# Step size of a state-space layer: the predicated copy stays on the Vector engine, the sum and the product move to GpSimd

## The reference

```
x = silu(causal_conv4(x_in))                    # 512 channels
dt, Bm, C = split(x @ x_proj_w.T)
dt = softplus(dt @ dt_proj_w.T + dt_proj_b)     # the step size
h = exp(dt * A) * h + dt * B * x                # 16 states per channel, over time
y = (h . C) + x * D ;  out = (y * silu(z)) @ out_proj_w.T
```

## Time and profile before

| what | value |
|---|---|
| time, median of 3 runs (lowest to highest) | 3368.63 us (3365.46 to 3370.95) |
| the profiled execution's own time | 3368.68 us |
| span in its trace, first to last instruction | 3367.0 us |
| busy: PE, DVE, ACT, POOL | 2878.9, 2203.8, 1425.5, 1199.6 us |
| mean granted TensorE clock | 0.909 of full speed |

### The profile page before, as it was taken

One profiled execution on the slowest core, in us unless ns is written; L12 is line 12 of the kernel. 1 busy time (PEld: TensorE's weight loads), 2 busy tenths in 40 slices (PEclk: granted clock), 3 DMA queues, 4 the chain that ended last, 5 costly groups with the idle time before them and its releaser, 6 DMA issues.

```text
span 3367.0 us, 45234 instructions
## 1 busy us (share of the span) xinstructions
PE 2878.9 (86%) x14054; PEld 1313.5 (39%) x14055; DVE 2203.8 (65%) x3070; ACT 1425.5 (42%) x2463; POOL 1199.6 (36%) x1360
## 2 busy tenths in 40 slices
PE   6994698888988988869999997878788888989876
PEld 5662133232332332236666665752222222222212
DVE  3576866766766767022222222646999999999997
ACT  2341065665655655712222221425445445545442
POOL 1143021221112212210000001825777767777675
PEclk9996598998988989979999998998898999998978
DMA  6166413133132130041111112620000000000000
GB/s 200 63 215 145 138 41 46 26 63 53 27 57 44 42 47 23 18 131 31 31 31 31 31 31 80 210 96 7 3 17 13 7 13 20 7 13 13 13 1 19
DMA packets 175061, 176.60 MB, mean 52 GB/s; under 512 B 50674, under 2 KB 151541, under 8 KB 174749
## 3 DMA queue, kind: packets, MB, share of 16 engines
q1 hardware_dynamic: 168732, 157.52, 18.7%
q0 software_dynamic: 6144, 16.82, 1.5%
HBM read 100.46 MB, written 73.83 MB: 52 GB/s over the span
## 4 chain that ended last, share of the span: by engine, by line
PE 50%; DVE 26%; issue 10%; ACT 5%; DMA 2%; POOL 2%; SPq 1%; another core or an unknown queue 1%; POOLq 0%; DVEq 0%; ACTq 0%; PEldq 0%
PE ps L1668 47%; DVE hh L1634 10%; DVE mp L1405 6%; DVE ps L1621 3%; POOL Ch L890 2%; PE ps L1876 2%; DMA ks<-qk_parts 1%; ACT Pt L1013 1%; DVE dt L1608 1%; DVE tl L1607 1%; DVE q L1317 1%; SPq L528 1%; PE ps L1832 1%; SPq L619 0%
## 5 line engine op out<-in xcount | busy, mean ns | idle before, releaser
L1405 DVE TENSOR_REDUCE mp<-ps 128x1 f32<-128x1024 f32 (+7 forms) x768 | 669.5, 909 | 276.0 <-PE ps L1668 245.7
L1013 ACT ACTIVATE Pt<-ps 128x512 f32<-128x512 f32 (+3 forms) x1280 | 611.6, 539 | 519.0 <-PE ps L1668 487.6
L890 POOL TENSOR_TENSOR Ch<-hh,Cb 128x1024 f32<-128x1024 f32 x256 | 603.7, 2358 | 72.6 <-DVE hh L1634 72.6
L1668 PE MATMUL ps<-ks,qs 96*128 96x512 bf16 (+3 forms) x1280 | 395.8, 382 | 117.8 <-DVE mp L1405 68.5
L1634 DVE TENSOR_TENSOR_SCAN hh<-dA,hst,ps 128x512 f32<-128x512 f32 x384 | 473.1, 1263 | 0.0
L766 POOL TENSOR_SCALAR_AFFINE_SELECT Pt<-Pt 128x128 f32<-128x128 f32 x512 | 147.8, 294 | 880.0 <-ACT Pt L1013 870.6
L1668 PE MATMUL ps<-dtx,pick 32*128 32x512 f32 x1024 | 326.0, 697 | 139.9 <-DVE hh L1634 139.1
L1668 PE MATMUL ps<-qs,ks 99*128 99x512 bf16 (+3 forms) x1280 | 413.3, 370 | 18.6 <-ACT Pt L1013 15.9
L1193 ACT ACTIVATE dA<-ps 128x1024 f32<-128x1024 f32 x256 | 261.8, 1023 | 392.4 <-PE ps L1668 392.1
L1621 DVE TENSOR_TENSOR ps<-ps,Bb 128x512 f32<-128x512 f32 x512 | 325.4, 680 | 32.9 <-PE ps L1668 32.4
L1668 PE MATMUL ps<-dt,WA 32*128 32x512 f32 x1024 | 322.0, 707 | 20.3 <-ACT dA L1193 20.1
(11 more groups left out here) (303 smaller groups left out, 3765.2 us busy)
## 6 DMA issues: line engine op xcount, KB each, us to landing
W<-in_L_ffn_w SPq DMA_DIRECT2D x16, 1024.0 KB, 12.0
qk_parts<-q SPq DMA_DIRECT2D x32, 384.0 KB, 2.9
qs<-qk_parts SPq DMA_DIRECT2D x96, 128.0 KB, 6.2
ks<-qk_parts SPq DMA_DIRECT2D x96, 128.0 KB, 8.7
expert_out<-yb SPq DMA_DIRECT2D x72, 128.5 KB, 2.5
expert_in<-zero SPq DMA_DIRECT2D x9, 1024.0 KB, 11.4
xg<-expert_in SPq DMA_DIRECT2D x72, 128.0 KB, 2.7
X<-in_L_attn_x SPq DMA_DIRECT2D x4, 1024.0 KB, 9.5
```

What stands on the lines that cost most here:

```text
L890: pool.tensor_tensor(Ch[:, k % 6, :, :], hh[:, k % HRING, :, :], Cb[:, par:par + 1, :].broadcast_to([P, 2, CH]), ALU.mult).then_inc(s_Ch, 1)
L1013: act.activation(Pt[:, n % PRING, q0:CH], ps[:, 4 + n % SRING, q0:CH], ACT.Exp, scale=SCALE).then_inc(s_exp, 1)
L1405: dve.tensor_reduce(mp[:, qc, h, t % TPC, k0 // 1024:k0 // 1024 + 1], slot[:, 0:n], AX.X, ALU.max).then_inc(s_free, 1)
L1668: return pe.matmul(o, lhsT, rhs, start=start, stop=stop, **kw)
```

## The change

`step_size` on the Vector engine shrinks to `select`, the predicated copy alone, at the same places. A new `step_size` on GpSimd does the sum and the product; it stands between the save of the state and the product with C in units 28, 0, 4, 8 (5, 9, 13 in chunk 0), and for the first block of all ahead of unit 0. A new semaphore `s_sel` goes from the one to the other. The three counters `s_nrm_abs`, `s_nrm_ps` and `s_sc`, each raised once, in that order, become one, `s_nrm`, awaited at 1, 2 and 3.

```diff
@@ GpSimd
+            def step_size(m, d):
+
+                par, b = m % 2, m * KI + d + 1
+                pool.wait_ge(s_sel, b)
+                pool.tensor_tensor(dt[:, par, d, :], dt[:, par, d, :], tl[:, d, :], ALU.add).then_inc(s_dt, 1)
+                pool.wait_ge(s_dt, b)
+                pool.wait_ge(s_xs, m + 1)
+                pool.tensor_tensor(dtx[:, par, d, :], dt[:, par, d, :], xs[:, par, d, :], ALU.mult).then_inc(s_dtx, 1)
...
             for step in range(2):
                 series(0, 0, step)
+            step_size(0, 0)
...
+                if n == 0 and u in (5, 9, 13):
+                    step_size(0, u // 4)
+                if n + 1 < NC and u == 28:
+                    step_size(n + 1, 0)
+                if n and u in (0, 4, 8):
+                    step_size(n, u // 4 + 1)
@@ ScalarE
-            act.activation(gb[:, :, :, :], ga[:, :, :, :], ACT.Abs).then_inc(s_nrm_abs, 1)
-
-            act.wait_ge(s_sc, 1)
-            act.wait_ge(s_nrm_ps, 1)
+            act.activation(gb[:, :, :, :], ga[:, :, :, :], ACT.Abs).then_inc(s_nrm, 1)
+
+            act.wait_ge(s_nrm, 3)
@@ Vector engine
-            def step_size(m, d):
-
-                par, b = m % 2, m * KI + d + 1
-                dve.wait_ge(s_mask, b)
-                dv.link(dve.copy_predicated(tl[:, d, :], te[:, d, :].bitcast(I32), dtx[:, par, d, :]))
-                dve.tensor_tensor(dt[:, par, d, :], dt[:, par, d, :], tl[:, d, :], ALU.add).then_inc(s_dt, 1)
-                dve.wait_ge(s_dt, b)
-                dve.wait_ge(s_xs, m + 1)
-                dve.tensor_tensor(dtx[:, par, d, :], dt[:, par, d, :], xs[:, par, d, :], ALU.mult).then_inc(s_dtx, 1)
+            def select(m, d):
+
+                dve.wait_ge(s_mask, m * KI + d + 1)
+                dve.copy_predicated(tl[:, d, :], te[:, d, :].bitcast(I32), dtx[:, m % 2, d, :]).then_inc(s_sel, 1)
```

More of the change, by code:

```diff
@@ L409, in build @@
         s_x, s_w, s_g = sem("s_x"), sem("s_w"), sem("s_g")
-        s_nrm_abs, s_nrm_ps, s_sc, s_scaled = sem("s_nrm_abs"), sem("s_nrm_ps"), sem("s_sc"), sem("s_scaled")
+        s_nrm, s_scaled = sem("s_nrm"), sem("s_scaled")
         s_hor, s_hev, s_sqp, s_sqe, s_fin, s_fev = (sem(n) for n in ("s_hor", "s_hev", "s_sqp", "s_sqe", "s_fin", "s_fev"))
@@ L445, in build @@
         s_jfull, s_jfree = sem("s_jfull"), sem("s_jfree")
-        s_xs, s_zs, s_ln, s_poly, s_mask, s_dt, s_dtx = (sem(n) for n in ("s_xs", "s_zs", "s_ln", "s_poly", "s_mask", "s_dt", "s_dtx"))
+        s_xs, s_zs, s_ln, s_poly, s_mask, s_sel, s_dt, s_dtx = (sem(n) for n in ("s_xs", "s_zs", "s_ln", "s_poly", "s_mask", "s_sel", "s_dt", "s_dtx"))
         s_dtb, s_dxb, s_dA, s_Bu, s_h, s_hst, s_Ch, s_red, s_yz, s_sum = (sem(n) for n in ("s_dtb", "s_dxb", "s_dA", "s_Bu", "s_h", "s_hst", "s_Ch", "s_red", "s_yz", "s_sum"))
@@ L1254, in _ @@
             dv = Chain(dve, c_dve)
-            dve.wait_ge(s_nrm_ps, 1)
+            dve.wait_ge(s_nrm, 2)
             dv.link(dve.tensor_reduce(nrm[:, 0:1], ps[:, 6:8, 0:512], AX.XY, ALU.max))
@@ L1260, in _ @@
             dv.link(dve.tensor_scalar(nri[:, 3:4], nri[:, 2:3], -1.0, 127.0, ALU.mult, ALU.add))
-            dve.tensor_single_scalar(nrm[:, 1:2].bitcast(I32), nri[:, 3:4], 23, ALU.logical_shift_left).then_inc(s_sc, 1)
+            dve.tensor_single_scalar(nrm[:, 1:2].bitcast(I32), nri[:, 3:4], 23, ALU.logical_shift_left).then_inc(s_nrm, 1)
             def statistics(k):
@@ L1643, in gate_y @@
                 dve.tensor_tensor(zs[:, n % 2, d, :], ps[:, 6, :], zs[:, n % 2, d, :], ALU.mult).then_inc(s_yz, 1)
-            step_size(0, 0)
+            select(0, 0)
             for k in range(NC * UNITS):
@@ L1650, in _ @@
                 if n == 0 and u in (5, 9, 13):
-                    step_size(0, u // 4)
+                    select(0, u // 4)
                 if n + 1 < NC and u == 28:
-                    step_size(n + 1, 0)
+                    select(n + 1, 0)
                 if n and u in (0, 4, 8):
-                    step_size(n, u // 4 + 1)
+                    select(n, u // 4 + 1)
                 if u in (11, 19, 27):
@@ L1674, in _ @@
             pe.wait_ge(s_const, 6 + TAYLOR)
-            pe.wait_ge(s_nrm_abs, 1)
+            pe.wait_ge(s_nrm, 1)
             for g in range(NROT + 1):
@@ L1678, in _ @@
                     last = mm(half(6 + g // 2, g % 2), ones_s[:, :], gb[:, min(g, NROT - 1), k, :], k == 0, k == KD - 1)
-            last.then_inc(s_nrm_ps, 1)
+            last.then_inc(s_nrm, 1)
             pe.wait_ge(s_scaled, 2)
```

## The result

The changed kernel takes 3340.45 us (median of 4 runs, 3336.55 to 3343.57); the kernel before, on the same chip, 3367.05 (3365.24 to 3370.95). The ratio is 0.9915, 95% interval 0.9903 to 0.9927: 0.85% or 27 to 29 us faster. Forecast were 45 us, with 3323 us as the likeliest time and 3300 to 3347 as the range. The direction and the place of the gain were right, its size was 1.5 to 1.7 times too large. The time lies inside the range, but 5 us above the 3307 to 3335 that had been given 60 in 100, and in the rival "half given back" (3335 to 3362).

A forecast was written before the change was run, and what follows sets the result against it. The Vector engine was taken as the bound, at 127 of 133 us in a chunk. 98.4 - 45.3 (copies) - 1.3 (start) - 3.5 (mask) - 3 (TensorE) = 45.3 us less, from 3368.7 to 3323 us; range 3300 to 3347.

The forecast's parts named there:

- the place of the gain: Last stage, Vector engine: taking sum and product, 69.8 us, from this bounding engine shortens the stage.
- half given back: Rival: new 3.4 us stall at unit 31 or 0 per chunk, or copies near 2.4 us; 3335 to 3362 us; 17 in 100.
- the counters: Three counters merged, one wait fewer on ScalarE: nothing won or lost that the measurement can tell (0.2%, 6.7 us).
- the mechanism of turns: Vector engine instructions with two SBUF inputs and GpSimd instructions reading SBUF exclude each other for their whole length.
- hidden waits for TensorE: TensorE loses 7 of its 18 us idle per chunk, so waits can surface; 3 us set, bounds nothing and 24.
- the slower rival: GpSimd becomes the bound through the ring of four `Ch`; some 3390 us; 4 in 100.
- the copy's term: Vector engine copies left: 24 at 1.6 us, seven of unit 28 at 0.88, the first 0.73; 45.3 us.
- full gain: Rival: copies stay near 0.8 us in gaps left by GpSimd's lag, nothing surfaces; 3293 to 3307 us; 15 in 100.
- a new stall of 3.4 us in each chunk: Second cause in a rival of 17 in 100: a stall at unit 31 or 0 of each chunk.
- The wait described for a short copy in unit 0: Unit 31's silu of z, covered by unit 0's 3.46 us step size; cover shrinks to 1.6; 0.4 us a chunk.
- The start: First block's step size, alone on the path: 2 x 0.69 becomes 2 x 1.27 and a hop between engines, +1.3 us.
- The mask: Block 3's mask waits for GpSimd's later half of unit 5, delaying unit 8's copy: 0.5 us in seven chunks, 3.5.

The follow-up runs named there:

- e3: Changed kernel without the predicated copy, its waits and signal kept; ratio 0.9833 to the kernel before, stage 1010.3 us.
- e9: Changed kernel without GpSimd's sum and product, only their signals kept; ratio 0.9837 to the kernel before, stage 1010.0 us.
- e4: Changed kernel with GpSimd's product with C as two instructions of 512 in every unit; ratio 0.9861 to the kernel before, stage 1020.1 us.
- e8: Changed kernel with the sum back on the Vector engine and GpSimd's product with C in two halves; ratio 0.9929 to the kernel before.

## Why the prediction was half right

Right: the counters (nothing); the place of the gain; both new instructions at 1.27 us; the mechanism of turns, by which a copy of 0.73 us waits out what GpSimd has begun; that GpSimd has hardly a pause from unit 28 to unit 8 (none between 2671.3 and 2723.0 us) but does not stop the scan (no wait of the scan for `Ch` in the trace after); that hidden waits for TensorE surface. Nothing in the trace speaks for the slower rival.

The step that failed is the size of the copy's term: "So a copy costs 0.72 + 0.88 = 1.6 us there. I take that for 24 copies". With the eight other copies it came to 45.3 us in the forecast; the trace has 59.0. The seven of unit 28 were as forecast but for one (0.74 to 1.69 us, together 6.7 against 6.2), the first 0.74; the 24 others took 51.5 us, 2.15 each in place of 1.6. I had taken the moment of the copy as random in a stretch in which GpSimd runs without a pause. It is not: ten of the 24 lie between 2.58 and 2.73 us, right behind the start of a product with C, the worst moment there is. The rival "full gain" had this objection in it, "the order of turns is fixed", with the wrong sign. Why the moment falls just there, right behind the start of a product, no run settles; one reason may be that both engines leave each collision together and then go through the same durations. The rival "half given back" came nearer: it named copies near 2.4 us. Its other cause, a new stall of 3.4 us in each chunk, did not come about as such.

Second, TensorE: 3 us were set, 9.4 measured, inside the bounds of 0 to 24. The wait described for a short copy in unit 0 appears in two of the seven chunks, 4 and 5, in units 3 and 4; these two make 6.5 of the 9.4 us. In chunk 5 the copy took 0.73 us, and the next units waited:

```profile
2941.89 0.73 DVE L1621 COPY_PREDICATED tl<-te,dtx 128x512 f32<-128x512 int32 x1
...
2954.19 0.69 DVE L1653 TENSOR_TENSOR zs<-ps,zs 128x512 f32<-128x512 f32 x1 [0.96 <-PE ps L1678]
...
2958.40 1.30 DVE L1631 TENSOR_TENSOR ps<-ps,Bb 128x512 f32<-128x512 f32 x2 [2.33 <-PE ps L1678]
```

In chunk 3, where it took 2.72 us, no wait follows in these units. But the copy's length does not decide it alone: in chunk 4 it took 2.29 us and 3.2 us of waits followed, in chunk 2 it took 2.22 us and none did. Why is open. As a sum, e3 and e9 show that copies cost less than they last: 59.0 us of them gone shorten the stage by 24.1, 30.7 gone by 24.4.

The two small terms were wrong to the safe side. The start cost nothing (first `drive` at 2301.74 us, before 2301.85): the Vector engine had waited there anyway, 4.68 us before and 6.13 after. The mask cost nothing (2.5 us of waits against 3.0). The slow copy of unit 8 seems to have covered it: in e4, where that copy took 1.2 us, it first waited 0.95 to 1.45 us for its mask in four of the chunks.

By the terms: 98.4 - 59.0 - 0 + 0.5 - 9.4 = 30.5 us in place of 98.4 - 45.3 - 1.3 - 3.5 - 3 = 45.3. The copy was 13.7 us too cheap and TensorE 6.4; start and mask were 5.3 us too dear and gave that much back, which was luck. Without it the time would still be inside the range, but by 1 us only.

## What to carry to other kernels

Before a Vector engine instruction with two SBUF inputs is moved to GpSimd, look at those that stay: here each copy waited until what GpSimd had begun was done, and the price of one collision went by the length of GpSimd's instruction (2.36 us, copies up to 2.73 in the changed kernel; in halves, e4, up to 1.83) more than by its load. Do not average over a schedule that repeats; walk it and expect the worst moment as readily as the best. Move one instruction at a time (here the product alone brought everything). Shorten the long instructions of the other engine where something stands behind them; where little did (e8), it did not help. Place what collides where that engine has caught up: in unit 15 the copy took 0.72 to 0.93 us.

## What the hardware showed that was not expected

Splitting GpSimd's 2.36 us product into two of 512 columns, more work for an engine that was already late, made the stage 14 us shorter (e4), because another engine's instruction of 0.73 us stood behind it in 21 of its 32 places. That much had been expected of e4 before it ran. Not expected was that the same split lengthened e8's stage by 10 us. The Trainium skill, page "SBUF — State Buffer", section "Who interferes with whom", says that the order of issue decides who blocks; the copy that came 0.24 us behind GpSimd's start and lasted 2.72 us agrees.
